# GELU expert mixture: the choice applied after the GELU by spread rows, in place of a mask product ahead of it

## The reference

```python
x = x + _L2_attn_ref(_layernorm(x), wq, bq, wk, bk, wv, bv, wo, bo)   # causal, one head of 64
x = x + _L2_ffn_ref(_layernorm(x), Wg, bg, W1, b1, W2, b2)

def _L2_ffn_ref(x, Wg, bg, W1, b1, W2, b2):      # H = 128, I = 128, E = 8 experts
    ...
    idx = jnp.argmax(jax.nn.softmax(xf @ Wg + bg, axis=-1), axis=-1)
    h = jax.nn.gelu(jnp.einsum('th,ehi->tei', xf, W1) + b1, approximate=False)
    y = jnp.einsum('tei,eih->teh', h, W2) + b2
    out = jnp.take_along_axis(y, idx[:, None, None], axis=1)[:, 0, :]
```

## Time and profile before

| | |
|---|---|
| Median of 3 runs | 1660.28 us (1652.94 to 1663.09) |
| Profiled execution: time | 1657.49 us |
| Profiled execution: span | 1655.8 us |
| TensorE busy over the span | 82% |
| VectorE, ScalarE, GpSimd busy | 59%, 49%, 30% |
| `causal_and_gelu`, from its first load to its last norm figures | 1056.2 to 1363.9 us |

### The profile page before, as it was taken

One profiled execution on the slowest core, in us unless ns is written; L12 is line 12 of the kernel. 1 busy time (PEld: TensorE's weight loads), 2 busy tenths in 40 slices (PEclk: granted clock), 3 DMA queues, 4 the chain that ended last, 5 costly groups with the idle time before them and its releaser, 6 DMA issues. The chain is left out here.

```text
span 1655.8 us, 22037 instructions
## 1 busy us (share of the span) xinstructions
PE 1350.8 (82%) x6868; PEld 746.3 (45%) x6868; DVE 984.1 (59%) x2722; ACT 804.6 (49%) x1604; POOL 503.6 (30%) x678
## 2 busy tenths in 40 slices
PE   5899999999973279456899989669999986999497
PEld 1233333333321169323455566445566554777332
DVE  7778888888825656358877843234334315554355
ACT  2567776777751035266555442124454433554244
POOL 3343334432100054484554533300000003221056
PEclk7799999999996579756999989759999996999799
DMA  5111111111026022100243234100000000000001
GB/s 149 49 49 40 40 52 48 39 47 52 21 70 146 0 51 63 36 24 14 67 74 63 52 53 103 34 3 4 7 4 4 4 1 19 2 1 1 13 20 32
DMA packets 76039, 64.27 MB, mean 39 GB/s; under 512 B 19323, under 2 KB 63563, under 8 KB 75923
## 3 DMA queue, kind: packets, MB, share of 16 engines
q1 hardware_dynamic: 72591, 57.15, 14.2%
q0 software_dynamic: 2304, 4.72, 1.2%
q10 hardware_dynamic: 1028, 0.98, 0.2%
HBM read 47.54 MB, written 13.79 MB: 37 GB/s over the span
## 5 line engine op out<-in xcount | busy, mean ns | idle before, releaser
L960 DVE TENSOR_REDUCE a_nm<-a_aps 128x1 f32<-128x512 f32 x512 | 333.4, 686 | 73.3 <-PE a_aps L725 73.2
L924 ACT ACTIVATE a_prob<-a_sps 128x512 f32<-128x512 f32 x512 | 271.3, 597 | 112.6 <-PE a_sps L737 111.7
L725 PE MATMUL a_aps<-a_K,a_Q 96*128 96x512 bf16 x512 | 193.4, 397 | 14.1 <-DMA a_K<-k_parts 12.5
L737 PE MATMUL a_sps<-a_Q,a_K 99*128 99x512 bf16 x512 | 155.9, 384 | 1.2 <-ACT a_prob L924 1.2
L1429 POOL TENSOR_TENSOR p_h<-p_sl,p_t 128x512 f32<-128x512 f32 x72 | 106.6, 1499 | 146.5 <-ACT p_sl L1569 60.0
L746 PE MATMUL a_ops<-a_prob,a_Vg 128*32 128x512 f32 x1024 | 135.7, 604 | 0.0
L725 PEld LDWEIGHTS a_aps<-a_K,a_Q 96*128 96x128 bf16 x512 | 50.2, 98 | 139.1 <-DVE a_nm L960 90.2
L1569 ACT ACTIVATE p_sl<-p_up_a 128x512 f32<-128x512 f32 x72 | 42.9, 597 | 113.9 <-PE p_up_b L1459 112.8
L1459 PE MATMUL p_up_b<-x_normT,p1w_w 128*128 128x512 f32 x144 | 76.1, 610 | 8.7 <-DVE p_t L1677 8.7
L434 POOL CAST a_ms<-a_mr 16x128 bf16<-16x128 f32 x32 | 9.0, 282 | 240.9 <-ACT a_mr L882 240.9
L737 PEld LDWEIGHTS a_sps<-a_Q,a_K 99*128 99x128 bf16 x512 | 49.9, 99 | 61.3 <-ACT a_prob L924 30.9
(11 more groups left out here) (525 smaller groups left out, 2687.2 us busy)
## 6 DMA issues: line engine op xcount, KB each, us to landing
p_G<-gates_by_expert SPq DMA_DIRECT2D x32, 512.0 KB, 8.9
a_Q<-q_parts SPq DMA_DIRECT2D x192, 32.0 KB
a_K<-k_parts SPq DMA_DIRECT2D x31, 96.0 KB
q_parts<-a_partsq SPq DMA_DIRECT2D x7, 384.0 KB, 2.8
k_parts<-a_partsk SPq DMA_DIRECT2D x7, 384.0 KB, 2.8
token_outputs<-m0e_y SPq DMA_DIRECT2D x40, 64.0 KB, 1.5
m0w_w<-in_L_ffn_W SPq DMA_DIRECT2D x1, 2048.0 KB, 9.2
m0w_w<-in_L_ffn_W SPq DMA_DIRECT2D x4, 512.0 KB, 10.0
```

The source lines that it names most:

```text
L725: nc.tensor.matmul(aps[n % 3][:, :], Q[0:MAX, head, q * P:(q + 1) * P], K[0:MAX, head, :], start=True, stop=True).then_inc(a_ready, 1)
L737: nc.tensor.matmul(sps[(NS * u + k) % 3][:, :], K[0:KB, head, k % TC * P:(k % TC + 1) * P], Q[0:KB, head, :], start=True, stop=True).then_ ...
L924: nc.scalar.activation(prob[u % 2][:, k // TC, k % TC, :], sps[n % 3][:, :], ACT.Exp).then_inc(p_done, 1)
L960: nc.vector.tensor_reduce(nm[u % 2][:, s:s + 1], aps[n % 3][:, :], AX.X, ALU.max, negate=True).then_inc(a_used, 1)
```

## The change

The mask product is gone, and `only` and `off` with it. Each `up` is the product with W1 alone, and the GELU runs over the unmasked sums. In its place:

- `ohT` is stored to a DRAM tensor `rows` of (8, 8, 512), and read back by four DMAs (512 KB each, two experts per DMA) that put each expert's row of 512 on all 128 partitions of the new tile `G`.
- `keep_chosen(c, e)` multiplies the GELU's result h by G in place. GpSimd does experts 0, 2 and 4, VectorE experts 1, 3, 5, 6 and 7. `down` waits for these in place of the GELU.
- `ohT` and `b2` are now 128 partitions high with zeros below row 8, so that the bias product of `down` has 128 rows.
- `up(s, 7)` stands ahead of `scores(s + 2)`.
- In filling, the product for `bc` no longer stands ahead of everything on TensorE but behind the first scores, and in step -1 `scores(1)`, `maxima(1)` and `exponentials(1)` stand behind `logits(0)`, `choose(0)` and `copy_choice(0)`.

```diff
+        rows = nc.dram_tensor("choice_rows", (B, E, S), FP, kind="Internal").ap()
-        ohT, off, h = two("ohT", [S], E), two("off", [S], E, BF), two("h", [E, S])
+        ohT, G, h = two("ohT", [S]), two("G", [E, S]), two("h", [E, S])
+        BY_POOL, BY_VECTOR = (0, 2, 4), (1, 3, 5, 6, 7)
...
+            def spread_choice(c):
+                sp.wait_ge(ohT_done, c + 1)
+                sp.dma_start(rows[c, :, :], ohT[c % 2][0:E, :]).then_inc(row_stored, 16)
+                wait_for(sp, pool_kept, c - 2, len(BY_POOL))
+                wait_for(sp, vector_kept, c - 2, len(BY_VECTOR))
+                sp.wait_ge(row_stored, 16 * (c + 1))
+                for i in range(E // 2):
+                    sp.dma_start(G[c % 2][:, 2 * i:2 * i + 2, :],
+                                 rows[c, 2 * i:2 * i + 2, :].unsqueeze(0).to_broadcast([P, 2, S])).then_inc(G_loaded[i], 16)
...
+            sp.wait_ge(rest_zeroed, 1)
+            sp.dma_start(b2[0:E, :], d["L2_ffn_b2"]).then_inc(e_loaded, 16)
+            for st in steps:
+                if here(st + 2):
+                    move_keys(st + 2)
+                if here(st + 1):
+                    spread_choice(st + 1)
...
+            def keep_chosen(c, e):
+                pool.wait_ge(h_done, E * c + e + 1)
+                pool.wait_ge(G_loaded[e // 2], 16 * (c + 1))
+                nc.gpsimd.tensor_tensor(h[c % 2][:, e, :], h[c % 2][:, e, :], G[c % 2][:, e, :],
+                                        ALU.mult).then_inc(pool_kept, 1)
...
                 if e == 0:
-                    pe.wait_ge(off_done, c + 1)
-                nc.tensor.matmul(hps[u % 2][:, :], only[:, e, :], off[c % 2][:, :], start=True, stop=False)
-                nc.tensor.matmul(hps[u % 2][:, :], W1[:, e, :], xT[c % 2][:, :], start=False, stop=True).then_inc(up_done, 1)
+                    pe.wait_ge(xT_done, c + 1)
+                nc.tensor.matmul(hps[u % 2][:, :], W1[:, e, :], xT[c % 2][:, :], start=True, stop=True).then_inc(up_done, 1)
 
             def down(c, k):
                 if k == 0:
-                    pe.wait_ge(h_done, E * (c + 1))
+                    pe.wait_ge(pool_kept, len(BY_POOL) * (c + 1))
+                    pe.wait_ge(vector_kept, len(BY_VECTOR) * (c + 1))
...
-                nc.scalar.activation(off[c % 2][:, :], ups[0:E, :], ACT.Copy, bias=-1.0).then_inc(off_done, 1)
-                nc.scalar.activation(ohT[c % 2][:, :], ups[0:E, :], ACT.Copy).then_inc(ohT_done, 1)
+                nc.scalar.activation(ohT[c % 2][0:E, :], ups[0:E, :], ACT.Copy).then_inc(ohT_done, 1)
```

More of the change, by code:

```diff
@@ L2069, in _ @@
                     up(s, 6)
-                if here(s + 2):
+                    up(s, 7)
+                if here(s + 2) and s + 1 != 0:
                     scores(s + 2)
+                if s + 2 == 0:
+                    pe.wait_ge(bvb_done, 1)
+                    pe.wait_ge(v_done, 1)
+                    nc.tensor.matmul(ups[:, 0:D], bvb[:, :], wo[:, :], start=True, stop=True).then_inc(bc_ready, 1)
                 if here(s):
-                    up(s, 7)
                     down(s, 0)
@@ L2082, in _ @@
                     logits(s + 1)
+                if s + 1 == 0:
+                    scores(s + 2)
                 if here(s):
                     down(s, 2)
+                if s + 1 == 0:
+                    turn_choice(s + 1)
                 if here(s + 2):
                     turn_prob(s + 2)
-                if here(s + 1):
+                if here(s + 1) and s + 1 != 0:
                     turn_choice(s + 1)
@@ L2288, in _ @@
                     normal_first(s + 3)
-                if here(s + 2):
+                if here(s):
+                    for e in (5, 6, 7):
+                        keep_chosen(s, e)
+                if here(s + 2) and s + 1 != 0:
                     maxima(s + 2)
+                if s + 2 == 0:
+                    v.wait_ge(bc_ready, 1)
+                    tt(bc[:, :], ups[:, 0:D], bo[:, :], ALU.add).then_inc(bc_done, 1)
                 if here(s + 1):
```

72 lines of the change are left out of this document (43 added, 29 removed).

## The result

The kernel after takes 1631.52 us (median of 4 runs, 1628.35 to 1632.97), the kernel before beside it 1657.85 (4 runs). The ratio is 0.9838, 95% interval 0.9801 to 0.9875: 1.6% faster, by between 1.2 and 2.0%. The forecast was 1639. The profiled execution took 1632.73 us, its span is 1631.0 against 1655.8: the stage starts 1.0 us later, is 27.4 us shorter, and what follows is 1.6 us longer.

What follows compares the result with a forecast made beforehand. TensorE's own work plus two waits was taken to bound the step. Six full steps give -17.1, step 6 -2.8, step 7 -2.0, filling +0.5, together -21.4: median 1639 us, range 1628 to 1653.

Steps and rivals of the forecast that it cites:

- five signs of being wrong: Waits on G's DMA; scores waiting for keys; VectorE products well over 0.7 us; clock under 1.00; step 0 over 2 us later.
- The masks: In each up on TensorE: a mask costs 0.32 us, the rest 1.05; eight per step give -2.5 us.
- the two banks make no new wait: In up: ScalarE's GELU of 0.69 us, with 0.1 to start it, still fits under a pitch of 1.05.
- The bias product: In each down: 128 rows in place of 8 take off 0.14 us, 0.56 per step; bounds 0 and 0.68.
- The wait ahead of the first down: On TensorE: the 0.78 us go in full steps; in steps 6 and 7 the wait is 1.6 us.
- The wait ahead of turn_second: On TensorE, for VectorE's chain from the scores: 1.55 us where 0.55 was, +1.0 per step.
- the third rival: VectorE and GpSimd block each other, products at 1.2 us each: a step saves 1.4, total 1648 us; chance 0.13.
- The rows: Transfers of G: a rate near 309 GB/s, all four DMAs done 9 us after first issue, in time in full steps.
- The first two rivals: Transfers of G: rows at 165 GB/s, 1657 us, chance 0.12; or slower still at 45 GB/s, 1775 us, chance 0.05.
- The rival of the slow rows: Transfers of G at 45 GB/s: eight chunks take 373 us, about 115 more than now, total 1775; chance 0.05.
- the term of +0.3: Step 7: rows are there at 9.1 us and needed at 8.2 to 9.3, a loss of some 0.3 us.
- Filling: Before step 0: keys 2.1 us earlier against weigh(1) 2.6 to 3.6 later; taken as +0.5 us.

Runs made afterwards that it cites:

- pad_both: Kernel before, masks kept, with the bias product and the mask product both made 128 rows high: 1638.21 us, ratio 0.9831.
- pad_bias: Kernel before, masks kept, with only ohT and b2 made 128 rows high (zeros below row 8): 1657.22 us, ratio 0.9939.
- norm_ahead: Kernel after with filling's old order, all products on VectorE, 128-row masks for the last chunk, and second norm ahead of the four maxima: 1620.66 us, ratio 0.9717.
- all_vector: Kernel after with all eight products of a chunk on VectorE and none on GpSimd: 1630.14 us, ratio 0.9774.
- mask_last: Kernel after with step -1 in the order of before and the last chunk alone done by 128-row masks: 1624.26 us, ratio 0.9747.

## Why the prediction was right, and where its terms were off

The total and the range held: 1631.52 us for the 1639 forecast. That owes something to luck: steps 0 to 6 gave 11.9 us more than forecast, filling and step 7 gave 5.9 less, and the errors offset. Of the five signs of being wrong that the prediction lists, four came: VectorE waited for G's DMA in step 7, its products took 1.01 us in the mean, the clock fell in step 7, and step 0 started 3.9 us later in the stage. A full step is 27.9 to 28.5, not 30. By its own steps:

- *The masks.* -2.5 per step was too small. The step that failed is "The mask costs 0.32 us, the rest 1.05": the rest was itself 0.19 dearer for standing behind a product of 8 rows (0.86 in pad_both). All in all a mask cost 1.37 - 0.94 = 0.43 us, eight of them 3.4. That the two banks make no new wait is wrong in small: the product with W1 alone takes 0.86 (1155.48 - 1154.62 in pad_both), and every second `up` waits for a GELU.
- *The bias product.* -0.56 forecast, -1.05 measured by pad_bias, outside its bounds of 0 to 0.68. I bounded only the two passes themselves (0.41 then, 0.22 now); the products beside them grow shorter too. It is the same mis-sizing as with the masks. Both together: pad_both shows 3.2 us per step from heights alone, which is more than the 2.85 that I gave the whole change. **The mechanism that carried the result was one that I had as a side term.**
- *The wait ahead of the first down.* -0.78 held, save for the steps in which blocking left 0.28; in step 6 the wait is 1.55 for the forecast 1.6. In step 7 it is 4.61, by the rows.
- *The wait ahead of turn_second.* Forecast 1.55, measured 1.22 or 1.55. That VectorE's chain from the scores is next was right, and norm_ahead shows that it was all of it.
- *The products, and the third rival.* The rival's mechanism is shown: 1.0 us per product, not 0.69. Its price was not: 1.45 per full step by the forecast (2.85 less 1.4), 0.44 in the mean measured against all_vector.
- *The rows.* The rate, at 330 to 400 GB/s, was above the 309 taken, and in time in full steps. The first two rivals fell with it. The issues took 1.74 us, not 3.21. The rival of the slow rows also had a slip in its sum: 373 us for eight chunks is about 129 more than the 244 that steps 0 to 7 took, not 115. In step 7 the term of +0.3 is a step that failed, since I compared the landing with each product's need one by one. But the products of a chunk queue: none could start before 1319.3, 5.8 us into the step, and from there eight of them on two engines in each other's way took 6.3 us. That, and the clock that fell in the gap, cost 3.9 us against mask_last.
- *Filling.* +0.5 forecast, +3.9 measured. The later `weigh(1)`, 1.7 us, is the chain of that paragraph, 3.3 (2.6 to 3.6 forecast), less 1.6 for the earlier start (2.1 forecast). The failed step is the clock: I weighed only that it might rise earlier. The new order puts a gap of 4.14 us in TensorE's row, the clock was still down at `weigh(1)`, and that cost 2.2 us more.
